# The order of step 0 in a recurrence over 16 steps: four small matmuls, a broadcast and the wait ahead of them

## What is computed

```python
xa = _ln(x, ln1_w, ln1_b)
sx = shifted(xa) - xa
xxx = xa + sx * maa_x
t = jnp.tanh(xxx @ maa_w1).reshape(B, L, 5, -1)
m = jnp.einsum('blfd,fdc->blfc', t, maa_w2)
mw, mk, mv, mr, mg = (m[:, :, j] for j in range(5))
xw = xa + sx * (maa_w + mw)      # the same for xk, xv, xr, xg
w = exp(-exp(time_decay + tanh(xw @ decay_w1) @ decay_w2))
r, k, v = xr @ Wr.T, xk @ Wk.T, xv @ Wv.T
g = silu(xg @ Wg.T)
def step(s, inp):                # over the 256 tokens
    a = k_l[..., :, None] * v_l[..., None, :]
    out = einsum('bhs,bhst->bht', r_l, faaaa * a + s)
    return a + w_l[..., None] * s, out
```

## Time and profile before

| | us |
|---|---|
| median of 3 runs | 3984.41 (3984.1 to 3984.75) |
| the profiled execution | 3986.14 |
| its span, first to last instruction | 3984.4 |
| TensorE busy | 3665.5 (92%) |
| VectorE busy | 2992.5 (75%) |
| ACT busy | 2030.6 (51%) |
| POOL busy | 1829.6 (46%) |

### The profile page before, as it was taken

One profiled execution on the slowest core, in us unless ns is written; L12 is line 12 of the kernel. 1 busy time (PEld: TensorE's weight loads), 2 busy tenths in 40 slices (PEclk: granted clock), 3 DMA queues, 4 the chain that ended last, 5 costly groups with the idle time before them and its releaser, 6 DMA issues. The chain is left out here.

```text
span 3984.4 us, 71128 instructions
## 1 busy us (share of the span) xinstructions
PE 3665.5 (92%) x21676; PEld 2809.6 (71%) x21676; DVE 2992.5 (75%) x6738; ACT 2030.6 (51%) x5166; POOL 1829.6 (46%) x1256
## 2 busy tenths in 40 slices
PE   7998999999999988999999878999999999999976
PEld 6777777778777777999999755666666666666643
DVE  6778777888888885665556557888888888888883
ACT  5777777777777775555455322333333333333321
POOL 5444444544444441000000036776777777777761
PEclk9999999999999998999999988999999999999988
DMA  5344443544444442000110300000000000000000
GB/s 152 95 105 111 109 102 95 149 116 126 121 124 111 112 133 98 32 32 32 33 46 32 108 28 20 25 25 25 25 25 25 25 25 25 25 25 25 19 19 16
DMA packets 143809, 256.54 MB, mean 64 GB/s; under 512 B 24384, under 2 KB 29248, under 8 KB 142624
## 3 DMA queue, kind: packets, MB, share of 16 engines
q1 hardware_dynamic: 143648, 254.48, 23.3%
HBM read 107.61 MB, written 33.55 MB: 35 GB/s over the span
## 5 line engine op out<-in xcount | busy, mean ns | idle before, releaser
L463 POOL TENSOR_TENSOR a_prob<-a_prob,a_rsums 128x512 f32<-128x512 f32 x512 | 541.6, 1060 | 780.9 <-DVE a_rsums L645 780.7
L1446 POOL TENSOR_TENSOR c_S<-c_S,c_rT 128x1024 f32<-128x1024 f32 x256 | 603.2, 2358 | 364.0 <-DVE c_S L1801 364.0
L535 ACT ACTIVATE a_prob<-a_t,a_tmin 128x256 f32<-128x256 f32 x1024 | 512.7, 501 | 363.8 <-DVE a_tmin L638 362.8
L1801 DVE TENSOR_TENSOR_SCAN c_S<-c_wT,c_vb 128x512 f32<-128x512 f32 x512 | 624.8, 1220 | 50.5 <-issue 8.6
L1796 DVE TENSOR_TENSOR c_vb<-c_kT,c_vb 128x510 f32<-128x510 f32 x512 | 350.8, 685 | 214.1 <-PE c_vb L2010 194.9
L634 DVE SCALAR_TENSOR_TENSOR a_ps_s<-a_ps_s,a_mask 128x512 f32<-128x512 f32 x512 | 357.2, 698 | 172.1 <-PE a_ps_s L741 103.6
L638 DVE CUSTOM_DVE_ANT_0 a_t<-a_ps_s,a_mneg 128x256 f32<-128x256 f32 x1024 | 394.1, 422 | 60.0 <-issue 0.7
L751 PE MATMUL a_ps_t<-w_ident,a_prob 128*128 128x128 f32 x2048 | 324.1, 282 | 27.2 <-ACT a_probT L545 17.5
L2010 PE MATMUL c_vb<-c_vhl,c_spread 128*128 128x512 f32 x512 | 283.1, 572 | 54.1 <-DVE c_S L1801 38.1
L741 PE MATMUL a_ps_s<-a_stack 96*128 96x256 f32 x1024 | 230.7, 308 | 82.6 <-DMA a_stack<-a_parts_qk 64.2
L545 ACT COPY a_probT<-a_ps_t 128x512 f32<-128x512 f32 x512 | 288.2, 563 | 1.6 <-PE a_ps_t L751 1.6
(11 more groups left out here) (255 smaller groups left out, 10080.9 us busy)
## 6 DMA issues: line engine op xcount, KB each, us to landing
a_stack<-a_parts_qk SPq DMA_DIRECT2D x768, 128.0 KB, 2.4
x<-w_x_out SPq DMA_DIRECT2D x48, 512.0 KB, 2.8
w_x_in<-x SPq DMA_DIRECT2D x48, 512.0 KB, 3.9
w_x_out<-x SPq DMA_DIRECT2D x32, 512.0 KB, 3.5
w_x_in<-in_x SPq DMA_DIRECT2D x16, 512.0 KB, 3.5
w_x_out<-in_x SPq DMA_DIRECT2D x16, 512.0 KB, 3.5
a_enc<-in_ctx SPq DMA_DIRECT2D x16, 512.0 KB, 4.4
b_xb<-x SPq DMA_DIRECT2D x16, 512.0 KB, 4.2
```

Source lines behind the costliest of these rows:

```text
L463: nc.gpsimd.tensor_tensor(prob[:, h % 4, :, :], prob[:, h % 4, :, :], rsums[:, h, :].unsqueeze(2).to_broadcast([P, TC, T]), ALU.mult).then ...
L535: op = nc.scalar.activation(prob[:, n % 4, tc, :], t[:, n % 2, tc, :], ACT.Exp, bias=tmin[:, n, tc:tc + 1], scale=-1.0, accum_out=psums[:, ...
L1446: nc.gpsimd.tensor_tensor(S[:, n % 4, :, :], S[:, n % 4, :, :], rT[:, par, :, :], ALU.mult).then_inc(z_ready, 1)
L1801: nc.vector.tensor_tensor_scan(flat(pair(S[:, n % 4, :, :], i)), flat(pair(wT[:, par, :, :], i)), flat(x), 0.0, ALU.mult, ALU.add).then_in ...
```

## The change

It does three things. mw0 and mk0 go from the first list of step 0 to the second, so that TensorE issues the broadcast of half 1 of step 0 first, and VectorE reads the two behind half 0 of step 1. mw0 waits for a new semaphore, `wk_ready`, which ACT raises behind the second of the five tanh. The old wait, for all five, goes to mr0, in step 4 (step 5 in pass 0).

```diff
-    FILLS = {0: (["mw0", "mk0"], ["mw1", "mk1"]), 1: (["g0"], ["y0", "y1"]), 2: (["g1", "dec1"], []), ...
+    FILLS = {0: ([], ["mw0", "mk0", "mw1", "mk1"]), 1: (["g0"], ["y0", "y1"]), 2: (["g1", "dec1"], []), ...
...
+        wk_ready = sem("wk_ready")
...
                             op = nc.scalar.activation(tT[row:row + DM, place, :], channels(k, name)[...],
                                                       ACT.Tanh)
+                            if n == "k":
+                                op.then_inc(wk_ready, 1)
...
                 def fill_together(k, name, second):
 
+                    if name == "mr0":
+                        pe.wait_ge(emptied["act"], units_0.emptied(k + 2, "Xt") if first(k) else units.emptied(k + 1, "t"))
                     if name == "mw0":
-                        pe.wait_ge(emptied["act"], units_0.emptied(k + 2, "Xt") if first(k) else units.emptied(k + 1, "t"))
+                        pe.wait_ge(wk_ready, k + 2)
                         pe.wait_ge(mix2_loaded, 16 * NMIX)
                         pe.wait_ge(bias_ready, 1)
```

More of the change, by code:

```diff
@@ L1098, in phase_c @@
     MIX_0 = ("k", "w", "r", "v", "g")
-    FILLS = {0: (["mw0", "mk0"], ["mw1", "mk1"]), 1: (["g0"], ["y0", "y1"]), 2: (["g1", "dec1"], []), 3: (["k0"], ["k1"]), 4: (["zT0", "zT1", "mr0", "mv0"], ["mr1", "mv1"]), 5: ([], ["o0"]), 6: (["o1"], ["r0", "r1"]), 7: (["mg0", "dec20"], []), 8: (["bonus0"], ["bonus1", "xcT0", "xcT1"]), 9: (["mg1", "dec21"], ["v0"]), 10: ([], ["v1"]), 11: (["kk0"], []), 12: (["kk1"], ["rr0"]), 13: (["xaT0", "xaT1"], ["rr1"]), 14: (["kv0"], ["kv1"]), 15: ([], ["t"])}
+    FILLS = {0: ([], ["mw0", "mk0", "mw1", "mk1"]), 1: (["g0"], ["y0", "y1"]), 2: (["g1", "dec1"], []), 3: (["k0"], ["k1"]), 4: (["zT0", "zT1", "mr0", "mv0"], ["mr1", "mv1"]), 5: ([], ["o0"]), 6: (["o1"], ["r0", "r1"]), 7: (["mg0", "dec20"], []), 8: (["bonus0"], ["bonus1", "xcT0", "xcT1"]), 9: (["mg1", "dec21"], ["v0"]), 10: ([], ["v1"]), 11: (["kk0"], []), 12: (["kk1"], ["rr0"]), 13: (["xaT0", "xaT1"], ["rr1"]), 14: (["kv0"], ["kv1"]), 15: ([], ["t"])}
     FILLS_0 = {0: ([], ["Xt"]), 1: (["g0"], ["mw0", "mk0"]), 2: (["mw1", "mk1"], ["g1"]), 3: ([], ["dec1", "k0"]), 4: ([], ["k1"]), 5: ([], ["mr0", "mv0"]), 6: (["mr1", "mv1"], []), 7: ([], ["r0"]), 8: ([], ["r1"]), 9: (["y0", "y1"], ["v0"]), 10: (["bonus0"], ["bonus1", "mg0", "dec20"]), 11: (["v1"], ["mg1", "dec21"]), 12: (["zT1", "o0", "o1"], ["xcT0", "xcT1", "kk0", "kk1", "rr0"]), 13: (["xaT0", "xaT1"], ["rr1"]), 14: (["kv0"], ["kv1"]), 15: ([], ["t"])}
```

## The result

| | us, median | against before, 95% interval |
|---|---|---|
| before | 3984.40 | |
| with the change | 4018.65 | 1.0088 (1.0070 to 1.0105) |

The change makes the kernel 34 us slower; the forecast was 25 us slower. The profiled execution took 4018.4 us, with a span of 4016.6.

What follows compares the result with a forecast made beforehand. TensorE was taken to bound each pass until VectorE leads late in it. Without the clock +1.3 us, plus 23.8 for the low clock, gives +25.1 us: 4009.5 against 3984.4 us (+0.6%), range 3990 to 4032.

Steps and rivals of the forecast that it cites:

- Part 1: Mixes on TensorE: waiting on two tanh lets mw0 and mk0 start 1.15 us earlier; the second pair can't.
- part 2: Broadcast of half 1 on TensorE goes right behind half 0's, at 2933.8 instead of 2936.69; VectorE had waited 1.01 us.
- Part 3: VectorE reads mw0 later, so g0 waits for its bank: next broadcast -0.87 us in pass 6, +1.82 in pass 7.
- the sum without the clock: Nine passes like pass 6 and five like pass 7, with g0 at full clock: 9 x (-0.87) + 5 x 1.82 = +1.3 us.
- The branch: VectorE stands 2.02 then 1.38 us behind the loop's branch, making passes 3, 5, 7, 9 and 11 +1.82 us each.
- Part 4: Half clock on TensorE from g0 on, after the stall: between 0 and 3.4 us a pass, 1.7 taken, 23.8 in 14.
- L: Time the low clock takes from g0 on, per pass: 1.7 us taken, bounds 0 and 3.4.
- (a): Rival: low stretch wholly behind the stall ahead of g0, or a second fall: +43 us or more, 4030; chance 0.10.
- (b): Rival: low clock doesn't come or ends inside the stall ahead of g0: +1.3 us, 3986, not slower; chance 0.12.
- (c): Rival: no clock cost and VectorE's standing behind the branch hidden, all 14 passes like pass 6: -12 us, 3972; chance 0.06.
- (d): Rival: second pair's bank wait holds the first mixes; same time within 0.2 us a pass, counted inside the forecast's 0.72.

Runs made afterwards that it cites:

- the third experiment: Changed kernel's TensorE order and wait, but VectorE reads mw0 and mk0 at the old place, behind half 1 of step 0: 3950.65 us, 0.9912 of before.
- the shifted loop: Changed kernel with pass 1 written out and the loop over passes 2 to 11, so its branch precedes passes 4, 6, 8 and 10: 4013.68 us.
- the wait alone: Changed kernel with mw0 and mk0 back ahead of the second broadcast, keeping the wait on two tanh: 3952.72 us, 0.9917 of before.
- the order alone: Kernel before with all four mixes behind the second broadcast in step 0, mw0 still waiting for all five tanh: 4021.48 us, 1.0094 of before.

## Why the prediction was right, and where its sizes were off

**Part 1 and part 2** came as worked out. The mixes start 0.86 us behind the first tanh (before: 1.97), the second pair follows without a gap, since the bank of t comes free just then, and the broadcast of half 1 goes out 0.34 us behind that of half 0. What the early broadcast is worth by itself these runs don't settle.

**Part 3** is the cause, and is shown: the wait of g0 is for the read of mw0, it follows VectorE's order (the read at its old place takes it away, one addition less shortens it by one addition), and it is gone with TensorE's order and wait unchanged. The forecast start of g0 was 8.21 us behind the first tanh in plain passes and 10.93 in pass 7; measured, it is 8.29 in pass 6 and 10.95 in pass 7. Over the 14 passes the sum without the clock is +1.7 us where I had +1.3. It is made from the time between the first tanh and the broadcast of half 1 of step 1: 175.5 us in total before; after, the starts of g0 sum to 130.0, and 14 x 3.37 us are 47.2 (3.37 us lie between g0 and that broadcast at full clock, 2928.08 to 2931.45 in the third experiment), so 177.2. That the sum is so close is luck in part. Two of the nine plain passes were not like pass 6, and the earlier trace rows had shown their low stretches before: pass 1 with 3.3 us and more had the broadcast at 10.9 us, pass 4 with 10.0 us and more at 14.1, where pass 6 has 12.5. Without the clock they give +1.2 and -2.4 us for the -0.87 of the forecast, and the two errors nearly cancel.

**The branch** was read rightly as one of the code, as the shifted loop shows. That it does nothing in the kernel before is the best lesson of this case about cover.

**Part 4, L.** The broadcast of half 1 of step 1 goes out 205.7 us behind the first tanh in total, so the low clock takes 205.7 - 177.2 = 28.5 us, 2.04 us a pass; I had taken 1.7. This is the term that was most undersized, by 4.7 us in all. It takes 1.4 to 3.0 us in a pass, always inside the bounds. The low stretches came as 3.4, 6.8 and 10.2 us; the long ones lie in branch passes and begin in or just behind the first of the two stalls, so that most of their length costs nothing. The 1.7 us was a middle of bounds and not a reading; that it was only 0.3 us a pass off is luck in part.

**The step that was missed** is the sentence that passes 15 and 16 have no mixes. Pass 15 has none, but it has g0. VectorE goes through the names of the mixes all the same, with a drain and an increment for each at the place of its read, and g0 waits for the one of mw0. TensorE in pass 15, before and then after:

```profile
3826.60 1.94 PE L2021 MATMUL c_acc<-c_S,c_gather 128*32 128x512 f32 x8
3828.47 5.33 PE L1889 MATMUL c_ps<-c_xmix,c_Wg 128*128 128x256 f32 x16
3833.44 0.58 PE L2010 MATMUL c_vb<-c_vhl,c_spread 128*128 128x512 f32 x1
```

```profile
3854.59 1.94 PE L2027 MATMUL c_acc<-c_S,c_gather 128*32 128x512 f32 x8
3858.91 6.23 PE L1893 MATMUL c_ps<-c_xmix,c_Wg 128*128 128x256 f32 x16 [2.38 <-DVEq L1747]
3864.79 0.58 PE L2016 MATMUL c_vb<-c_vhl,c_spread 128*128 128x512 f32 x1
```

From the start of acc to the broadcast it is 6.84 us before and 10.20 after: 3.4 us more, which the forecast had at nothing.

**The balance**: 1.7 + 28.5 + 3.4 = 33.6 us, against 32.2 between the spans. The very first tanh came 2.1 us earlier in the span of after (2278.1 for 2280.2). It lies ahead of all that the change touches, and over the eleven traces it lies between 2276.9 and 2280.3. So 34.3 us are to be explained, and the rest of under 1 us I leave open.

**The rivals.** (a) asked for the low stretch to lie wholly behind the stall; in the four plain passes with 6.8 us of low clock it nearly does (L of 2.8 to 3.0), in the others it doesn't. No second fall came later in a pass. (b) fell: the clock fell in all 14 passes. What stood beside it holds by itself, though: where the gap is filled or closed and no new one opens, the clock stays up, but for two of the nine plain passes of the wait alone. By that rule (the Trainium skill, TensorE: Matmul & The Clock Gate, Why this matters for your kernels: gaps between bursts of matmuls bring the half clock back) the gap is what has to go; the filled gap agrees, with 29 us. The page means longer gaps than this one, though. The prediction's "the trace agrees" holds for the direction alone: by the runs here a gap of 1.58 us is already enough. (c) fell: the branch was not hidden in the changed kernel; five passes had g0 at 10.9 to 11.1 us. Had it been, the change would still have lost 18 us. (d) was no rival in time, as it said, and the order alone confirms that the start of the mixes is of no account there.

The sentence from the Trainium skill (Perfetto Trace Analysis, Optimization Strategy) on repeated gaps and too few PSUM buffers pointed to the right place: 49.0 us in 14 like gaps, each for a bank. That there are too few banks no run shows. With the same four banks and the read in its old place the wait is 6.2 us in 9 gaps, so what opened the gap is where VectorE reads, and not their number.

## What to carry to other kernels

Where one table sets the order on two engines, moving a step for the sake of one moves it on the other: look at what the other engine now does ahead of it, and at who waits for the buffer that it frees there; a wait that was met early is safe only if its margin is larger than the shift. Here the margin was 1.5 us, and an addition and a half step came in ahead of the read, 3.1 us. Ask the same of passes in which the moved step is only passed over. And price a short gap on TensorE by the clock of what follows it, not by its own length: here 1.6 us of standing cost 3.4 us more, and a filled gap cost nothing more. A delay of another engine that costs nothing today (the branch) can also become the bound as soon as its cover is made faster.

## What the runs showed of the hardware

Four matmuls with no use, 1.9 us of work while TensorE waited for the tanh, kept the granted clock at 1.00 in 14 of 14 passes where it had been 0.50 for 6.8 us in most, and made the kernel 29 us faster. VectorE stood about 2.0 us behind the loop's branch and, in the kernel before and the changed one, 1.4 us more at the next scan; in the shifted loop the second part was absent, and in code without a loop both were. What it stood for the traces don't say.
